# Second attention: the add of the sine products that transfers bring across, on VectorE at a unit's end in place of GpSimd

## The reference, cut to what matters

```python
q_hk = (hidden_q @ Wq.T).reshape(Bv, Sv, H, K)              # H = 16 heads
q_big = jnp.einsum('bshk,hkq->bshq', q_hk, w_kc_q)          # 192 columns a head
q_big = _apply_rope(q_big, sin_q[None, :, None, :], cos_q[None, :, None, :])
q_r = jnp.einsum('bshq,hqr->bhsr', q_big, W_qr)
k_r = jnp.einsum('bld,hdr->bhlr', kv_r, W_kr)
scores = jnp.einsum('bhsr,bhlr->bhsl', q_r, k_r)
attn = jax.nn.softmax(scores, axis=-1)
ctx_c = jnp.einsum('bhsl,bld->bhsd', attn, kv_r)
```

## Time and profile before

| | |
|---|---|
| median of three runs | 1338.18 us (1338.04 to 1339.47) |
| the profiled execution's own time | 1339.73 us |
| its span, first to last instruction | 1337.9 us |
| mean granted TensorE clock, as a share of full speed | 0.986 |
| busy: PE, DVE, ACT, POOL | 1264.2, 838.9, 715.2, 467.6 us |
| the second attention | from about 485 to about 885 us of the span |

### The profile page before, as it was taken

One profiled execution on the slowest core, in us unless ns is written; L12 is line 12 of the kernel. 1 busy time (PEld: TensorE's weight loads), 2 busy tenths in 40 slices (PEclk: granted clock), 3 DMA queues, 4 the chain that ended last, 5 costly groups with the idle time before them and its releaser, 6 DMA issues.

```text
span 1337.9 us, 27286 instructions
## 1 busy us (share of the span) xinstructions
PE 1264.2 (94%) x9584; PEld 989.3 (74%) x9584; DVE 838.9 (63%) x1986; ACT 715.2 (53%) x2746; POOL 467.6 (35%) x451
## 2 busy tenths in 40 slices
PE   5799999999999688999999999979999999999998
PEld 4678888888887564666666666557788888888887
DVE  6788888888888676666666656765443433434333
ACT  2788888888887653344444444464232332423322
POOL 3122113112211135345454534641153353533532
PEclk9899999999999999999999999999899999999999
DMA  6002000200012101102102101200323342154230
GB/s 221 16 18 57 18 17 18 57 17 17 22 28 92 31 17 63 55 23 77 47 17 92 32 17 33 76 1 1 110 63 139 71 123 55 39 137 78 55 95 31
DMA packets 34737, 72.78 MB, mean 54 GB/s; under 512 B 7872, under 2 KB 12992, under 8 KB 33344
## 3 DMA queue, kind: packets, MB, share of 16 engines
q1 hardware_dynamic: 34624, 71.32, 19.5%
HBM read 52.29 MB, written 2.23 MB: 41 GB/s over the span
## 4 chain that ended last, share of the span: by engine, by line
PE 75%; DVE 9%; ACT 8%; issue 4%; POOL 2%; DMA 1%; SPq 0%; DVEq 0%; POOLq 0%; ACTq 0%
PE ps L553 32%; PE ps L945 9%; PE ps L669 5%; PE ps L842 4%; PE ps L701 4%; PE ps L738 3%; ACT ea L1456 3%; PE ps L832 3%; PE ps L692 3%; PE ps L814 2%; PE ps L822 2%; PE ps L608 2%; ACT ea L1500 2%; DVE ea L1094 1%; PE ps L683 1%
## 5 line engine op out<-in xcount | busy, mean ns | idle before, releaser
L1828 POOL TENSOR_TENSOR sg<-sg,cw 128x512 f32<-128x512 f32 x88 | 113.7, 1292 | 260.5 <-ACT sg L1619 254.0
L1397 DVE TENSOR_TENSOR hh<-ps,sg 128x512 f32<-128x512 f32 x100 | 69.2, 692 | 179.1 <-POOL sg L1828 161.4
L1423 ACT ACTIVATE hhh<-hh 128x512 fp32r<-128x512 f32 x100 | 63.4, 634 | 214.5 <-DVE hh L1397 214.5
L1423 ACT ACTIVATE pt<-ps 128x512 f32<-128x512 f32 x128 | 77.0, 601 | 182.0 <-PE ps L822 124.6
L1456 ACT ACTIVATE ea<-ps,negmax 128x64 f32<-128x64 f32 (+1 forms) x512 | 165.0, 342 | 6.7 <-DVE negmax L1149 6.7
L1196 DVE TENSOR_TENSOR qcs<-ps,tabb 128x512 f32<-128x512 f32 x192 | 123.6, 686 | 55.3 <-PE ps L553 54.9
L553 PE MATMUL ps<-xnh,wch 128*128 128x512 f32 x400 | 157.3, 393 | 0.7 <-ACT pt L1423 0.7
L553 PE MATMUL ps<-xnl,wch 128*128 128x512 f32 x400 | 157.1, 393 | 0.0
L553 PE MATMUL ps<-xnh,wcl 128*128 128x512 f32 x400 | 155.6, 389 | 0.0
L1687 POOL TENSOR_TENSOR ea<-ea,rden 128x128 f32<-128x128 f32 (+1 forms) x128 | 62.3, 508 | 263.0 <-DVE rden L1105 263.0
L1694 POOL TENSOR_TENSOR eb<-eb,rsum 128x512 f32<-128x512 f32 x64 | 67.4, 1054 | 183.6 <-DVE rsum L1240 183.4
(11 more groups left out here) (154 smaller groups left out, 3337.1 us busy)
## 6 DMA issues: line engine op xcount, KB each, us to landing
raw_w<-in_rawb_dram SPq DMA_DIRECT2D x4, 2432.0 KB, 9.0
kva<-ktmp SPq DMA_DIRECT2D x64, 128.0 KB, 2.3
kvt<-qcs SPq DMA_DIRECT2D x64, 128.0 KB, 2.3
cw<-comb_d SPq DMA_DIRECT2D x32, 256.0 KB, 4.9
raw_w<-in_rawc_dram SPq DMA_DIRECT2D x4, 1920.0 KB, 8.2
cw<-comb_d SPq DMA_DIRECT2D x16, 224.0 KB, 4.8
raw_a<-in_wqk_dram SPq DMA_DIRECT2D x4, 768.0 KB, 5.7
cw<-comb_d SPq DMA_DIRECT2D x16, 192.0 KB, 5.7
```

What stands on the lines that cost most here:

```text
L1397: dve.tensor_tensor(hh[:, par, :], bank(C_U[par]), sg[:, par, :], ALU.mult).then_inc(c_h, 1)
L1423: return act.activation(dst, src, ACT.Copy)
L1828: pool.tensor_tensor(sg[:, par, :], sg[:, par, :], cw[:, c % 2, t, :], ALU.mult).then_inc(c_hs, 1)
```

## The change

The add of the crossed sine products goes from GpSimd to VectorE: the same instruction, with the same operands, now in `b_ends`. It stands at the end of the chunk's second unit on VectorE, behind slot 2; for the very first chunk of the first group it stands one unit later, at the end of u = 2. The one ahead of the first group stands behind the drain of the first attention, ahead of `ln_stats(2 * NC - 1)`. It counts a semaphore of its own, `b_er`, for which PE's step 0 waits; steps 1 and 2 wait for `b_rp`, which now counts the two ropes of a chunk alone. The instruction runs 16 times in all, before and after.

```diff
             def b_contract(g_to, c, n, steps):
 
                 q = g_to * NC + c
-                pe.wait_ge(b_rp, XT // 2 * q + (1 if steps[0] == 0 else 3))
+                if steps[0] == 0:
+                    pe.wait_ge(b_er, q + 1)
+                else:
+                    pe.wait_ge(b_rp, 2 * q + 2)
...
+            def b_ends(g_to, c):
+
+                dve.wait_ge(b_sw, 64 * (g_to * NC + (c + 1)))
+                dve.tensor_tensor(qcs[:, 0:2, 0, :], qcs[:, 0:2, 0, :], qsw[:, :, :], ALU.add).then_inc(b_er, 1)
+
             def b_unit(g, u, first=False, final=False, drain=False):
...
                     add_x((u - 3) % UN, b_wo, n - 3, b_y)
                 slot(2)
+                c = u // CB
+                if not drain and u % CB == (2 if first and c == 0 else 1) and not (final and c == NC - 1):
+                    b_ends(g + 1 if c == NC - 1 else g, (c + 1) % NC)
                 if first and u == 2:
                     ln_low(2 * NC - 1)
...
+            b_ends(0, 0)
             ln_stats(2 * NC - 1)
             dve.wait_ge(a_wo, NG * UN)
...
-            def tails(g_to, c):
-
-                pool.wait_ge(b_sw, 64 * (g_to * NC + (c + 1)))
-                pool.tensor_tensor(qcs[:, 0:2, 0, :], qcs[:, 0:2, 0, :], qsw[:, :, :], ALU.add).then_inc(b_rp, 1)
-
             def b_rope(g, u, final=False):
 
                 c = u // CB
                 if final and c == NC - 1:
                     return
-                if u % CB == 1:
-                    tails(g + 1 if c == NC - 1 else g, (c + 1) % NC)
...
-            tails(0, 0)
             rope(0, 0, 0, XT + 3)
```

More of the change, by code:

```diff
@@ L263, in decoder_kernel @@
         b_rp, b_qs, b_sw = sem("b_rope_added"), sem("b_qr_ready"), sem("b_sines_crossed")
+        b_er = sem("b_end_rows_added")
         b_sc, b_mx, b_ex = sem("b_scores"), sem("b_negmax"), sem("b_exp")
```

## The result

The changed kernel takes 1345.23 us, the median of 6 runs (1344.4 to 1346.04), where the kernel before took 1338.11 us beside it, also in 6 runs (1337.25 to 1339.54). The ratio is 1.0049, with a 95% interval from 1.0037 to 1.006: 7.1 us slower, and well beyond the 0.2% that a measurement can tell from nothing. The forecast was 1345.7 us.

What follows compares the result with a forecast made beforehand. PE bounds the kernel (three quarters of the span), so only its waits count. Eleven chunks 6.25, passage 1.05, `wco` chunks 0 and first chunk 0.2 sum to 7.5 us: 1338.18 + 7.5 = 1345.7 us, range 1340 to 1348.5.

Steps and rivals of the forecast that it cites:

- VectorE beside GpSimd: In the steady chunks `b_ends` waits for GpSimd's running rope and ends 1.07 us behind it.
- The 0.76 us and the room of 0.15: Eleven chunks: take 0.76 us late, room 0.15, scores 0.61 late; 6.25 us in sum.
- The `wco` chunks: Three chunks, second unit of groups 1 to 3: 1.2 us of room take the 0.76, cost 0.
- The passage: From first to second attention: `b_ends(0, 0)` delays the takes PE waits for, +1.05 us; both PE waits grow.
- the clock's extra: In the passage: longer idling of PE might cost up to 1 us more by a lower clock; taken as 0.
- The first chunk: Second attention's first chunk: the `norm` wait goes, but step 0 and `obl` wait for VectorE; +0.2 us.
- The lower bound: First chunk: -2.6 us, if step 0 starts 1.0 us earlier and the slow-clock matmuls run at full speed.
- The sum: Whole span: 6.25 + 1.05 + 0 + 0.2 = 7.5 us slower.
- No blocking: Rival: take only 0.1 us late, eleven chunks free, passage costs 1.1, first chunk gains 1.0; about 1338.3; 10%.
- The second rope: Rival, eleven chunks: GpSimd's second rope goes ahead of `b_ends`, scores 1.9 us late, 1360; 4%.
- The faster rival: No blocking, first chunk's unit at full clock (-2.6), passage's 1.05 covered by the rope wait; 1335.6; 3%.

Runs made afterwards that it cites:

- The reductions without a tile: Kernel before plus an unread VectorE reduction at fourteen places, result written into `den`: 1339.02 us with 1024 columns, 1344.95 us with 1664.
- twin halves: The changed kernel with its add split into two instructions of 512 columns: 1363.34 us, ratio 1.0187.
- the kernel with all together: Adds on VectorE right behind slot 1's take, the passage's add on GpSimd, statistics behind the takes: 1331.08 us, ratio 0.9947 to the kernel before.

## Why the prediction was right, step by step

**VectorE beside GpSimd.** Shown. The working had `b_ends` in the chunk of the earlier trace rows from 667.2 to 669.07; the trace has it from 669.42 to 671.33, and that less 2.22 is 667.20 to 669.11. The blocking was read from two rows of half the columns and doubled, 1.07 us; measured 1.09. The ropes that wait for `b_ends` show that the order of starting decides, both in the changed kernel (`b_ends` behind L1772, ahead of L1773) and with the add moved (ahead of L1772).

**The 0.76 us and the room of 0.15.** Shown: 0.79 and 0.61 in the chunk above, 0.61 or 0.62 in all eleven. Behind the last of them PE gave back 0.35 of it, where I had counted three quarters, 0.46. The term was 6.25 and measured 6.7 - 0.35 = 6.4. The reductions without a tile test this from the other side, with the same stall at nearly the same length (0.59 at 1.88 us).

**The `wco` chunks.** 0 expected, 0.05 to 0.06 each found. The 1.2 us of room shrank to 0.50, and twin halves overran it.

**The passage.** The timeline of the changed kernel, against the earlier trace rows:

```profile
502.44 0.42 DVE L1114 TENSOR_TENSOR x_sb<-ps,x_sb 128x256 f32<-128x256 f32 x1 [0.67 <-PE ps L702]
...
502.78 1.23 DVE L1220 TENSOR_TENSOR qcs<-qcs,kvt 128x1024 f32<-128x1024 f32 x1
...
505.85 2.48 DVE L1200 TENSOR_TENSOR qcs<-ps,tabb 128x512 f32<-128x512 f32 x4
...
507.29 1.63 PE L742 MATMUL ps<-qcs,mq 64*64 64x512 f32 x8 [2.14 <-DVE qcs L1200]
...
511.04 3.65 PE L742 MATMUL ps<-qcs,mq 64*64 64x512 f32 x16 [2.12 <-POOL qcs L1773]
...
521.16 0.66 PE L561 MATMUL ps<-idf,xnt 128*128 128x128 f32 x4 [0.31 <-ACT xnh L1436]
```

Step 0 starts 4.85 us behind the `x_sb` add in place of 3.83, +1.02 for the 1.05 of the sum. PE's first wait grew from 1.12 to 2.14. One part of the step was wrong: the second wait, for the rope, did not grow but shrank, from 2.67 to 2.12. The first eight matmuls took 1.63 us in place of 1.09, with the clock already down, so PE arrived later at the second wait. By the scores of unit 0 it is +1.10, so the clock's extra, which I took as 0 with a bound of 1, was 0.1. By those of unit 2 it is +1.41. This further 0.31 is not the clock but a term that the sum did not have: the last row is a wait of PE for ScalarE's `xnh` in unit 1, which the kernel before does not have, and which stands with the same 0.31 in the two kernels whose statistics come later, where the clock read 1.00 throughout the passage.

**The first chunk.** This term had the wrong sign: +0.2 in the sum, -0.67 measured. The order of work came out as it was worked out. In the changed kernel's timeline:

```profile
530.06 2.08 DVE L1220 TENSOR_TENSOR qcs<-qcs,kvt 128x1024 f32<-128x1024 f32 x1
...
531.01 2.25 POOL L1677 TENSOR_TENSOR xnl<-xnf,xnh 128x512 fp32r<-128x512 f32 x1
...
532.19 1.09 PE L742 MATMUL ps<-qcs,mq 64*64 64x512 f32 x8 [1.82 <-DVE qcs L1220]
...
534.29 0.65 PE L836 MATMUL ps<-pt,kvr 128*64 128x256 f32 x4 [1.01 <-DVE obl L1237]
...
535.78 1.95 PE L742 MATMUL ps<-qcs,mq 64*64 64x512 f32 x16
```

This stretch is 0.41 us later in the span than in the kernel before. Less that, `b_ends` ends at 531.7, step 0 starts at 531.8 and L836 at 533.9, each as predicted. What failed is the speed of what follows. Step 0's eight matmuls took 1.09 us and not the 1.78 of the earlier trace rows, and from step 0 to step 1 it was 3.59 us instead of 4.07. The granted clock, in the kernel before and then in the changed one:

```profile
531.00:533.00 2.00, 1.61 (x12) 0.62 (x12) 0.45 (x2) 0.92 (x4) 2.00 (x3) 0.81 0.84 263
533.00:535.00 2.00, 2.00 (x9) 0.56 (x6) 0.00 (x0) 1.22 (x8) 2.00 (x3) 0.50 1.01 428
```

```profile
531.00:533.00 2.00, 0.81 (x8) 0.21 (x8) 2.00 (x2) 0.00 (x1) 2.00 (x2) 1.00 0.97 243
533.00:535.00 2.00, 0.99 (x9) 0.35 (x6) 1.83 (x4) 0.22 (x1) 0.35 (x2) 1.00 0.93 399
```

I had set the wait for `norm` against the new wait for `b_ends` and kept the clock. Why the clock stayed up is not shown. That there are now two shorter waits (1.82 and 1.01 us) in place of one of 2.02 does not explain it: with the passage's add on GpSimd it fell behind the same 1.82, and with two halves it stayed at 1.00 behind a single wait of 2.96. The lower bound had this case, but at -2.6 with step 0 a microsecond earlier.

**The sum.** 6.4 + 1.4 + 0.2 - 0.7 = 7.3 us in the trace, against 7.5: the passage and the `wco` chunks 0.5 more, the eleven chunks 0.1 more, the first chunk 0.9 less. So the closeness of the total is in part luck: the errors have different signs, and the largest hangs on the clock. With the first chunk as it came out with the passage's add on GpSimd, +1.9 in place of -0.7, the sum would have been 9.9.

**The rivals.** No blocking (1338.3) is refuted by the 1.90 us, and the kernel whose ropes wait shows what it would have been like: 1339.5, the passage's cost less the first chunk's gain. The second rope did not get in ahead in the changed kernel (that would have cost 22 us); it did with two halves, where VectorE gave it an opening. The faster rival is not this change's; the kernel with all together shows that its two parts, no blocking and a first chunk at full clock, were to be had by another order.

## What to carry to other kernels

What moving an elementwise add from GpSimd to VectorE cost was set by what GpSimd did at that moment, not by VectorE's busy share: with two SBUF inputs, VectorE waited for GpSimd's running instruction (1.90 us in place of 1.22). Put such an add where GpSimd is still idle, or let GpSimd, which has time, be the one that waits; and don't split it. Before that, measure the room of the chain behind it: here 0.15 us of room turned 0.76 us into 0.61 eleven times, and 1.2 us of room hid it but for 0.05.

## What the runs showed of the hardware that was not expected

- A tile of 64 bytes a partition that nothing uses cost 0.26% (1.0017 to 1.0036), by matmuls that were one to five nanoseconds longer. An experiment that adds a tile compares two layouts; the same work written into an old tile cost nothing (0.9996). Open: which of the moved tiles it is.
- The clock of one and the same stretch came out differently from kernel to kernel. In the first chunk it read 1.00 throughout in the changed kernel and with the ropes waiting, with the add behind slot 1 and with two halves (10.12 to 10.20 us each), and 0.50 for six microseconds with the passage's add on GpSimd (12.69), though its instructions there are those of the changed kernel. With the kernel before's own program it took from 10.78 to 11.72 us in six profiles (that of the kernel before, the four with reductions and the one with the tile), and 12.55 with the statistics behind the takes. So the cause of the miss with the passage's add is shown as far as the clock, and what made the clock fall there is not settled: by small shifts ahead of the stretch, or by chance from one execution to the next, as there is one profile of each kernel. The length of PE's wait alone does not decide it (fallen behind 1.82 us, up behind 2.96).
